# First mixture of a two-layer network on one core: turned rows' high halves ahead of the silu, low halves ahead of its product

## What is computed

```python
logits = normed @ router_w.T
top_v, top_i = jax.lax.top_k(jax.nn.softmax(logits, axis=-1), 2)
gates = jax.nn.softmax(top_v, axis=-1)
for e in range(8):
    gate, up = jnp.split(normed @ gate_up_w[e].T, 2, axis=-1)   # 768 each
    y = (jax.nn.silu(gate) * up) @ down_w[e].T                  # 768 -> 256
    out = out + comb[:, e, None] * y
```

## Time and profile before

| what | value |
|---|---|
| median of 3 runs (lowest to highest) | 2284.33 us (2282.07 to 2284.67) |
| the profiled execution: its time, its span | 2285.36 us, 2283.6 us |
| busy share of the span: TensorE, VectorE, ScalarE, GpSimd | 92%, 77%, 59%, 28% |
| first mixture's loop over tiles, first to last silu | 509.5 to 1010.7 us |
| TensorE's granted clock in the span, of full speed | 0.964 |

### The profile page before, as it was taken

The page is one execution under the profiler, slowest core; times in us unless marked ns, Lnnn a source line. Parts: engine busy times, 40 slices in busy tenths (PEclk is TensorE's granted clock), DMA queues, the critical chain, the costliest instruction groups (busy, mean ns, idle before and its releaser), DMA issues.

```text
span 2283.6 us, 49026 instructions
## 1 busy us (share of the span) xinstructions
PE 2110.7 (92%) x18242; PEld 1300.2 (57%) x18242; DVE 1754.0 (77%) x3080; ACT 1345.6 (59%) x2561; POOL 635.2 (28%) x761
## 2 busy tenths in 40 slices
PE   6999999879999999985876999999999999999998
PEld 5888886545566666654653333344434434448886
DVE  4677767646666666657989899989989998936878
ACT  6787785215554444433331899888888898862110
POOL 1000000102333333333554233533443343322000
PEclk9999999999999999997886899999999999998999
DMA  5445435651222222223333010101101111100000
GB/s 183 156 136 172 143 135 208 212 205 32 52 38 38 38 40 40 38 35 140 132 138 135 29 63 30 42 32 51 40 34 51 36 38 42 60 20 10 19 19 28
DMA packets 92485, 176.46 MB, mean 77 GB/s; under 512 B 16496, under 2 KB 64624, under 8 KB 90592
## 3 DMA queue, kind: packets, MB, share of 16 engines
q1 hardware_dynamic: 78624, 154.57, 19.4%
q0 software_dynamic: 13632, 18.77, 5.0%
HBM read 105.99 MB, written 66.78 MB: 76 GB/s over the span
## 4 chain that ended last, share of the span: by engine, by line
PE 50%; DVE 17%; issue 5%; ACT 5%; DMA 2%; SPq 1%; POOL 0%; DVEq 0%; POOLq 0%; ACTq 0%
PE PS L2354 11%; DVE NM L2235 7%; PE PS L58 7%; PE PS L60 6%; PE PS L59 6%; PE PS L2436 6%; PE PS L2379 5%; DVE TT L1716 2%; DVE X L2626 2%; PE PS L2374 2%; PE PS L2307 1%; ACT CW L1089 1%; ACT HB L1089 1%; DMA x_resid<-YI,IDX 1%; DVE CW L1298 1%
## 5 line engine op out<-in xcount | busy, mean ns | idle before, releaser
L2235 DVE TENSOR_REDUCE NM<-PS 128x2 f32<-128x1024 f32 (+3 forms) x608 | 678.8, 1161 | 59.3 <-PE PS L2379 54.9
L2140 ACT ACTIVATE E<-PS 128x512 f32<-128x512 f32 (+2 forms) x1280 | 634.6, 554 | 115.6 <-PE PS L2436 106.6
L2354 PE MATMUL PS<-E,VP 128*32 128x256 f32 (+1 forms) x5120 | 364.7, 370 | 1.5 <-ACT OT L2172 1.1
L2072 POOL TENSOR_SCALAR_AFFINE_SELECT E<-E 128x512 f32<-128x512 f32 x256 | 161.9, 634 | 292.2 <-ACT E L2140 292.1
L2354 PEld LDWEIGHTS PS<-E,VP 128*32 128x32 f32 x5120 | 110.0, 109 | 147.6 <-issue 109.8
L2436 PE MATMUL PS<-QK 50*128 50x512 f16 (+3 forms) x1152 | 184.9, 331 | 4.2 <-DVE X L2259 2.1
L58 PE MATMUL PS<-WALL,XIH 128*128 x426 | 163.7, 384 | 20.5 <-DVE HB L1298 7.5
L2379 PE MATMUL PS<-QK 48*128 48x512 f16 (+3 forms) x1152 | 172.9, 338 | 7.4 <-DVE NM L2235 7.4
L1105 ACT ACTIVATE HB<-HB,SCH 128x768 f32<-128x768 f32 x71 | 66.4, 935 | 177.5 <-DVE SCH L1312 177.5
L999 POOL DMA_INDIRECT XB<-x_normed,IDX x71 | 70.9, 998 | 354.8 <-PE PS L1465 285.6
L59 PE MATMUL PS<-WALL,XIH 128*128 x426 | 163.4, 384 | 0.0
(11 more groups left out here) (366 smaller groups left out, 4426.1 us busy)
## 6 DMA issues: line engine op xcount, KB each, us to landing
WIN<-in_we SPq DMA_DIRECT2D x24, 768.0 KB, 4.6
parts<-PP SPq DMA_DIRECT2D x32, 512.0 KB, 3.0
WALL<-pairs_of_weights SPq DMA_DIRECT2D x7, 2304.0 KB
QK<-parts SPq DMA_DIRECT2D x96, 128.0 KB
pairs_of_weights<-WPH SPq DMA_DIRECT2D x24, 384.0 KB, 2.4
pairs_of_weights<-WIN SPq DMA_DIRECT2D x24, 384.0 KB, 3.1
QK<-parts SPq DMA_DIRECT2D x96, 64.0 KB
values<-VS SPq DMA_DIRECT2D x8, 576.0 KB, 3.4
```

The costliest lines, as they stand in the source:

```text
L2072: e.affine_select(out=E[:, m % NE, :, 0:128], in_=E[:, m % NE, :, 0:128], pattern=[[0, 4], [1, 128]], compare_op=ALU.is_ge, fill=0.0, base ...
L2140: e.activation(dst, src, ACT.Exp, scale=unit).then_inc(S.ex, 1)
L2235: e.tensor_reduce(dst, src, AX, ALU.max).then_inc(S.mx, 1)
L2354: a = e.matmul(PS[32 * jj:32 * jj + 32, 7, 512 - n + c0:512 - n + c1], VP[b % 2][:, kt, 17 * hd:17 * hd + 32], E[:, m % NE, jj, c0:c1], st ...
```

## The change

In each of the passes, ScalarE makes the high halves of tile s - 1's turned rows before the silu of tile s instead of after it, and VectorE their low halves before the product of tile s instead of after it. No instruction, wait or buffer is added or removed.

```diff
--- before.py
+++ after.py
@@ -1092,14 +1092,14 @@
         for s in range(NT + 1):
             if s + 1 < NT:
                 high(s + 1)
+            if s > 0:
+                turned_high(s - 1)
             if s < NT:
                 gu = PS[:, 3 * (s % 2):3 * (s % 2) + 3, :].rearrange("p k s -> p (k s)")
                 e.wait_ge(S.pe_up, s + 1)
                 if s > 0:
                     e.wait_ge(S.hh, s)
                 e.activation(SI[:], gu[:, 0:768], ACT.Silu, scale=UN[:, 0:1]).then_inc(S.si, 1)
-            if s > 0:
-                turned_high(s - 1)
             if s < NT:
                 e.wait_ge(S.scl, s + 1)
                 e.activation(HI, HI, ACT.Copy, scale=SCL[:, 0:1]).then_inc(S.hs, 1)
@@ -1339,6 +1339,8 @@
                 turned(s + 1)
             if s in (8, 9):
                 lengths(s)
+            if 0 < s <= NT:
+                turned_low(s - 1)
             if s < NT:
                 gu = PS[:, 3 * (s % 2):3 * (s % 2) + 3, :].rearrange("p k s -> p (k s)")
                 e.wait_ge(S.si, s + 1)
@@ -1347,8 +1349,6 @@
                 else:
                     e.wait_ge(S.m_st1, nth(7))
                 e.scalar_tensor_tensor(out=HI, in0=gu[:, 768:1536], scalar=UN[:, 0:1], in1=SI[:], op0=ALU.mult, op1=ALU.mult).then_inc(S.hh, 1)
-            if 0 < s <= NT:
-                turned_low(s - 1)
             if s < NT:
                 row_scale(s)
             if s > 1:
```

## The result

| | before | changed |
|---|---|---|
| median of 14 runs each (lowest to highest) | 2284.64 us (2282.07 to 2288.03) | 2289.93 us (2286.40 to 2293.43) |
| profiled execution, its span | 2285.36, 2283.6 | 2291.22, 2289.5 |

The ratio is 1.002, 95% interval 1.0013 to 1.0027. The change makes the kernel slower by 5.3 us between the medians (3.0 to 6.2 us by the interval), where 6.8 were forecast.

A forecast was written before the change was run, and what follows sets the result against it. TensorE's 0.32 wait for low halves gives way to YI. Regular passes +3.8, row lengths -0.6, first pass -0.4, late DMAs +2.1, table load +1.2, tail +0.7: +6.8, 2292.2 profiled, median 2291.1 us; range 2281.5 to 2297.5.

The forecast's parts named there:

- The mechanism: First mixture's loop: YI replaces the low halves as TensorE's last wait; passes of 7.12 us, 0.06 more; chance 0.55.
- One sign: VectorE in the loop: YI's waits for the accumulating DMA stay unchanged, in ten passes, but now cost time.
- The link with a rival: VectorE, product to maximum: 1.06 us; the rival took 0.93, for passes of 6.99 to 7.06, chance 0.18.
- The first pass: First loop pass with low halves: waits for them and not for YI, 2.07 - 1.65, so -0.4 us.
- Tail: Loop's end: last maximum 0.68 later, with YI and the last accumulating DMAs behind it: +0.7 us.
- table load: Thirteenth pass: the silu's load of 1.28 falls between high halves and silu, on YI's chain: +1.2 us, bounds 0 and 2.1.
- late passes: Nine passes where YI waits for the accumulating DMA: lateness no longer hidden by slack, +2.1 us, bounds 0 and 3.3.
- The slack of the low halves: TensorE's first rows: low halves allow a start at 2.53, TensorE is ready at 2.63, so 0.10 to spare.
- such a drain: ScalarE, thirteenth pass: by the skill some 1.38 us behind the load, costing 1.4 more; the rows show none.

The follow-up runs named there:

- `before_pad_l`: Kernel before, plus an unused VectorE maximum of about 0.94 us ahead of YI in passes 15 to 63: 2290.74 us in one run.
- `after_early_yi3`: Changed kernel with YI moved ahead of the maximum and three YI buffers instead of two: 2261.88 us (4 runs), ratio 0.9916.
- `after_preload`: Changed kernel with the silu's table loaded in pass 12 right behind the side task's exponential, ahead of XIH: 2288.53 us (10 runs), ratio 1.0017.

## Why the prediction was right

- **The mechanism** was the forecast's: YI, with 0.63 of slack, became the last to arrive. Every link came out within 0.01, `before_pad_l` gives the slack, and `after_early_yi3` gives back the whole gain when YI is moved. One sign did not come: YI's waits for the DMA were to stay as they were, and went from ten to three.
- **The link with a rival**, the maximum behind the product's own semaphore, is 888.74 - 887.69 = 1.05 in each pass, not 0.93; with 0.93 the pass would have been 6.99. The sentence of the Trainium skill (VectorE: DVE Perf Modes, The DRAIN you can't avoid) that a semaphore "costs nothing extra" doesn't hold for this pair. It was good to take the one row with the same neighbours over the many with others.
- **The first pass** was mis-sized, -0.4 for -2.2 in the traces. The step priced a shorter wait by its length alone and didn't ask what the clock does after it.
- **Tail and table load** came out a little dearer (+1.0 for 0.7, +1.7 for 1.2), late passes too (+2.5 for 2.1, of which the DMAs are the 2.1). The +1.7 holds a clock that fell in both kernels and that the forecast didn't have. These terms and the first pass cancel in part: that the sum of 6.8 came so near the 5.3 measured is partly luck.
- **The slack of the low halves**, 0.10, held: TensorE's first rows never waited in regular passes. The silu started at the load's end in pass 13 (608.40 after 607.11 + 1.28) with no drain behind it. The prediction weighed the figure of the Trainium skill (ScalarE: Activation LUTs, What ACT_TABLE_LOAD costs) for such a drain; this trace doesn't show one.

## What to carry to other kernels

When a wait is taken from the bound engine, list every other wait that this engine has in the same period, with the slack of each, and take both from it: the delay of the chain behind, and the time by which the engine now comes earlier. Here 0.68 + 0.32 - 0.63 = 0.37 of new waiting stood against the 0.32 that was saved. The 0.32 is in both, so the sign hung on 0.68 of delay against 0.63 of slack. Slack that is used up also stops hiding whatever was irregular, such as late DMAs and table loads; and an instruction that nobody waits for soon (the maximum) should not stand ahead of one that the bound engine waits for (YI), if its buffer's DMA lets it go earlier.

## What the hardware showed that was not expected

- A wait of TensorE shorter by half a microsecond (1.6 for 2.1 us) in the loop's first pass went with a granted clock of 1.00 where it had fallen (0.73 over the next 6.4 us): 1.7 us of clock beside 0.5 of waiting. One kernel kept it with the longer wait, so it isn't certain in each execution.
- The same was seen around the late YI of pass 12. Up to there the changed kernel and `after_preload` have the same order; in the traced execution of the first YI's DMA landed later and the clock fell, in that of the second it didn't, and pass 12 differs by 1.2 us for the DMA and 1.2 for the clock. Before a difference between two traces is put down to an edit, the granted clock of both belongs beside it.
- With the same 49026 instructions, the kernels here lie between 2262 us (with a third YI buffer) and 2402 us.
